# Loading the adjacency as int8 with converting GpSimd transfers, and a new split of the comparisons, in a graph-attention kernel

## The chip, the cores and the metric

The kernel runs on one core of one Trainium2 chip. The metric is device time in microseconds (us) of one execution. The kernel before takes 1601.66 us, the median of three runs (1600.64 to 1603.05). Its engines are TensorE (PE, with its weight loads apart as PEld), VectorE (DVE), ScalarE (ACT), GpSimd (POOL) and SyncE (SP), which here only issues transfers.

## The reference

One graph-attention layer with four heads of 32 outputs over 8192 nodes, then a residual and a layer norm without scale:

```python
Wh = (h @ W.T).reshape(n, K, OUT_DIM).transpose(1, 0, 2)      # n = 8192, K = 4, OUT_DIM = 32
e = jax.nn.leaky_relu(score_src + score_dst, 0.2)             # [K, n, n]
e = jnp.where((adj == 0)[None, :, :], -jnp.inf, e)
alpha = softmax(e, axis=-1)
h_prime = jnp.einsum('kij,kjd->kid', alpha, Wh)
x = _layernorm(x + h_prime.transpose(1, 0, 2).reshape(n, K * OUT_DIM), axis=-1)
```

`adj` is an int32 array of 8192 x 8192, whose values are 0 and 1 (268 MB; all of it must be read). `x` is 8192 x 128 fp32.

## The kernel before, in words

The exponential of a leaky ReLU of a sum splits into two products, one for a positive sum and one for a negative one. So no exponential is taken per edge: for every pair (i, j) and head only a bit is wanted, whether the sum is positive ("step") or not ("rest"), and the edge bit. TensorE then multiplies the step bits by table G and the rest bits by table F, both made once in the first 91 us.

**Tiling.** The rows i of the adjacency go in 16 groups of 512, and in each group the columns j in 16 "quads" of 512, 256 quads in all, numbered k. For one quad:

- SP loads the 512 x 512 block of int32 in two transfers of 128 partitions x 2 rows x 512 numbers (`load_adj`, L284) into one of two buffers `adj_t`. It waits for `edge_set`, which GpSimd raises when it has read that buffer.
- GpSimd turns the block into int8 with a clamp to -1..1 (`take_edges`, L351), into one of two buffers `edge`, and raises `edge_set`.
- TensorE transposes it (`transpose_edges`, 8 instructions, L770), two quads ahead of its use, into one of two PSUM banks, and raises `transposed`.
- The comparisons are 128x512 pieces, each with one head and one of four 128-row blocks. Heads 0 and 1 (`kept`, one of them kept from a group to the next) are ScalarE's alone: four instructions of double width (L471, 128x1024). Heads 2 and 3 make eight pieces, which `tiles(g, q)` deals out by `SHARES` as (ScalarE, GpSimd, VectorE): (2, 4, 2) in groups 1 to 14, (1, 5, 2) in group 0, (3, 4, 1) in group 15. ScalarE's are L471, GpSimd's L421, VectorE's L638.
- VectorE masks the step bits with the transposed edges (`take_step`: L650, L652 and L657; where it has a single piece of its own, L655 and L657) and makes the rest bits (`take_rest`: L665, L667). It makes its comparisons of quad k + 1 between the two.
- TensorE adds 64 products with G, then the transposes of quad k + 2, then 64 products with F (all L783), and raises `rest_done`.

**What sets the order.** Every engine's program is written out by hand, and semaphores couple them. GpSimd and ScalarE may be up to three quads ahead of TensorE (`NS = 3`, they wait for `rest_done`). VectorE's `take_step` waits for all three sharers of the quad. In GpSimd's program a quad is: its comparisons, `take_edges` for the quad two ahead, and in nine of the sixteen quads of a group one piece of closing work on the group before (`close` L363 to L387 and `inverse_deviation` L391). VectorE's closing work is `finish`, ScalarE's are L498 (accumulators copied out after quad 1) and L504. GpSimd's part of a quad:

```python
for n, h in tiles(g, q)[1]:
    last = nc.gpsimd.tensor_scalar(step_u8[...], s_own[...], STEEP, d_steep[...], ALU.mult, ALU.add)
last.then_inc(pool_compared, 1)
if k + N8 < GROUPS * QUADS:
    take_edges(k + N8)
if q in CLOSING and g > 0:
    close(g - 1, CLOSING.index(q))
```

Of the kernel before, what the change touches and what calls it, by code (L numbers as in the profile page):

```python
# [6 lines left out]
def gat_layernorm(nc, x, adj, W, a, out):  # L7
# [31 lines left out]
    JB = N // P  # L39
    XT = N // ROWS  # L40

    NA = 2
    N8 = 2
    NS = 3
    KEPT = 2
    PLACES = QUADS + NS
# [20 lines left out]


    TILES = [(0, 3), (1, 3), (0, 2), (1, 2), (2, 2), (3, 2), (2, 3), (3, 3)]
    SHARES = ((2, 4, 2),)  # L70

    def tiles(g, q):
        first_or_last = {0: (1, 5, 2), GROUPS - 1: (3, 4, 1)}
# [17 lines left out]
    with ctx:  # L91
# [8 lines left out]
        F = sb("F", [P, JB, HEADS, FP, HC], fp16)  # L100
        s_two = sb("s_two", [P, KEPT, 2, ROWS], fp32)
        s_own = sb("s_own", [P, 2, HEADS - KEPT, ROWS], fp32)
        adj_t = sb("adj_t", [P, NA, IB, ROWS], i32)
        edge = sb("edge", [P, N8, IB, ROWS], i8)
        kept = sb("kept", [P, PLACES + NS, WORDS], i32)
        step = sb("step", [P, NS, HEADS - KEPT, WORDS], i32)
# [89 lines left out]
        G1_set = sem("G1_set")  # L196
        G2_set = sem("G2_set")
        f_set = sem("f_set")
        adj_loaded = [sem(f"adj_loaded{n}") for n in range(NA)]
        edge_set = sem("edge_set")  # L200
        transposed = sem("transposed")
        act_compared = sem("act_compared")
        pool_compared = sem("pool_compared")
# [53 lines left out]
        @block.sync  # L257
        def _(sync):
            sync.sem_inc(stored, 16 * LEAD)
            sync.dma_start(w_sb, W[:, :]).then_inc(w_loaded, 16)  # L260
            for side in range(2):
                sync.dma_start(a_col[:, side:side + 1], a[:, side * D_OUT:(side + 1) * D_OUT].rearrange("h (c o) -> h c o", o=1)
                               ).then_inc(w_loaded, 16)
            for t in range(XT):
                sync.dma_start(blocks(x_sb[:, t]), x_v[t]).then_inc(x_loaded[t], 16)

            def load_s(g, h, to, loaded):
                sync.dma_start(to, sT_v[g, h].unsqueeze(0).to_broadcast([P, ROWS])).then_inc(loaded, 16)

            def load_own(g, h):  # L270
                load_s(g, h, s_own[:, g % 2, h - KEPT], own_loaded[g % 2])

            def load_two(g, later):

                if g + later < GROUPS:
                    load_s(g + later, g % 2, s_two[:, g % 2, 1 - later], two_loaded[g % 2])

            def load_adj(g, q):

                k = quad_no(g, q)  # L280
                if k >= NA:
                    sync.wait_ge(edge_set, k - NA + 1)
                for u in range(U):
                    sync.dma_start(adj_t[:, q % NA, u * E:(u + 1) * E], adj_v[g, q, :, u]).then_inc(adj_loaded[q % NA], 16)  # L284

            def store_rows(g):
                sync.wait_ge(y_set, done(g + 1))
                sync.dma_start(o_v[g], blocks(y)).then_inc(stored, 16)

            def load_rows(g):  # L290

                if g == 0:
                    sync.wait_ge(rest_done, QUADS)
                else:
                    sync.wait_ge(stored, 16 * done(g))
                sync.dma_start(blocks(y), x_v[g]).then_inc(res_loaded, 16)

            for g in range(GROUPS):
                for q in range(QUADS):
                    load_adj(g, q)  # L300
                    if g == 0 and q + 1 == NA:
                        for n in range(2):
                            sync.wait_ge(s_copied, n + 1)
                            sync.dma_start(sT_rows[n], s_rows[:, n]).then_inc(s_stored, 16)
                        sync.wait_ge(s_stored, 32)
                        load_s(0, 1, s_first, first_loaded)
                        load_two(0, 0)
                        load_two(0, 1)
                        load_own(0, 2)
                        load_own(0, 3)  # L310
                    if q == 4 and g > 1:
                        store_rows(g - 2)
                    if q == 7 and g > 0:
                        load_rows(g - 1)
                    if q in S_QUADS and g + 1 < GROUPS:

                        if g == 0:
                            sync.wait_ge(wide_set, UNITS)
                        else:
                            sync.wait_ge(rest_done, quad_no(g, 0))  # L320
                        n = S_QUADS.index(q)
                        if n < 2:
                            load_two(g + 1, n)
                        else:
                            load_own(g + 1, n)
            store_rows(GROUPS - 2)
            load_rows(GROUPS - 1)
            store_rows(GROUPS - 1)
            sync.wait_ge(stored, 16 * done(GROUPS))

        @block.gpsimd
        def _(pool):
# [10 lines left out]
            nc.gpsimd.affine_select(out=identf, in_=identf, compare_op=ALU.not_equal, fill=1.0,  # L343
                                    base=0, pattern=[[-1, P]], channel_multiplier=1).then_inc(consts_set, 1)

            def take_edges(k):

                pool.wait_ge(adj_loaded[k % NA], 16 * U * (k // NA + 1))
                if k >= N8:
                    pool.wait_ge(transposed, k - N8 + 1)  # L350
                nc.gpsimd.tensor_scalar(edge[:, k % N8], adj_t[:, k % NA], 1.0, -1.0, ALU.min, ALU.max).then_inc(edge_set, 1)  # L351

            def close(g, part):

# [35 lines left out]
                pool.wait_ge(var_set, done(g + 1))  # L390
                nc.gpsimd.tensor_tensor(rstd[:, :], mv[:, :, 1], half_t[:, :], ALU.pow).then_inc(rstd_set, 1)  # L391

            for k in range(N8):
                take_edges(k)
            pool.wait_ge(d_part_set, 1)
            nc.gpsimd.partition_all_reduce(d_max[:, :], d_part[:, :], P, bass.bass_isa.ReduceOp.max).then_inc(d_max_set, 1)
            pool.wait_ge(d_part_set, 2)
# [16 lines left out]
            for g in range(GROUPS):  # L414
                pool.wait_ge(own_loaded[g % 2], 32 * (g // 2 + 1))
                for q in range(QUADS):
                    k = quad_no(g, q)
                    if k >= NS:
                        pool.wait_ge(rest_done, k - NS + 1)
                    for n, h in tiles(g, q)[1]:  # L420
                        last = nc.gpsimd.tensor_scalar(step_u8[:, k % NS, h - KEPT, n // E, :, n % E], s_own[:, g % 2, h - KEPT],  # L421
                                                       STEEP, d_steep[:, q * IB + n, h:h + 1], ALU.mult, ALU.add)
                    last.then_inc(pool_compared, 1)
                    if k + N8 < GROUPS * QUADS:
                        take_edges(k + N8)
                    if q in CLOSING and g > 0:
                        close(g - 1, CLOSING.index(q))
                    if q == 13 and g > 0:
                        inverse_deviation(g - 1)
# [298 lines left out]
        def _(pe):  # L728
# [34 lines left out]
                nc.tensor.transpose(tr[n][:, 0:P], sd[:, 0, n * JB // 2:(n + 1) * JB // 2, :].rearrange("p j h -> p (j h)"), identf  # L763
                                    ).then_inc(sT_psum, 1)

            def transpose_edges(q):

                for u in range(U):
                    for b in range(IB):
                        last = nc.tensor.transpose(edgeT16[q % 2][:, u, b * P:(b + 1) * P],  # L770
                                                   edge16[:, q % N8, b, u * P:(u + 1) * P], identb[:, :])
                last.then_inc(transposed, 1)

            def add_quad(q, matrices, values, width, first, before=None, after=None):
# [26 lines left out]
            def group(g):  # L801
                for q in range(QUADS):
# [8 lines left out]
                             G, BC, 0, before=(lambda b: open_bank(g, b)) if q == 0 else None)  # L811
                    pe.wait_ge(rest_set, k + 1)
                    if k + 2 < GROUPS * QUADS:
                        pe.wait_ge(edge_set, k + 3)
                        transpose_edges(q + 2)
                    add_quad(q, [rest_f8[:, k % NL, n] for n in [n for _, n in two] + list(range(KEPT, HEADS))], F, FC, BC, after=close_bank if q + 1 == QUADS else None
                             ).then_inc(rest_done, 1)

            pe.wait_ge(s_copied, 2)
            for k in range(2):  # L820
                pe.wait_ge(edge_set, k + 1)
                transpose_edges(k)
            pe.wait_ge(G2_set, UNITS)
            pe.wait_ge(f_set, UNITS)
# [23 lines left out]
```

## Time and profile before

| | |
|---|---|
| runs | 1600.64, 1601.66, 1603.05 us |
| profiled execution, first to last instruction | 1599.2 us (no time of its own is listed apart from this span) |
| granted TensorE clock, mean | 0.976 |
| busy share PE, PEld, DVE, ACT, POOL | 89%, 87%, 97%, 94%, 86% |
| DMA | 303 MB, 189 GB/s over the span |
| chain that ended last | ACT 48%, DVE 29%, PE 14%, issue 5%, POOL 4% |
| groups 1 to 14 | 92.4 us each, 5.78 us for a quad |

The profile covers one execution. "Busy" counts the time in which an engine has an instruction under way; instructions of one engine overlap at their ends by some 0.03 to 0.09 us, so the price of an instruction in a row of its kind is the distance between starts, a little less than its duration. Granted clock 1.00 is 2.4 GHz and 0.50 is 1.2 GHz. Transfers that SP issues are shown as SPq.

### The profile page before, as it was taken

Reading aid. Unit: us, or ns where it says so; the run is one execution under the profiler, and the core shown is the slowest. Engines: PE = TensorE matmul, PEld = TensorE weight load, DVE = VectorE, ACT = ScalarE, POOL = GpSimd, SP = SyncE. Lnnn points to the kernel's source line nnn. Section 1 sums busy time; section 2 is a strip of 40 time slices with the busy share of each in tenths; the row PEclk is TensorE's granted clock in tenths of the full one; section 3 lists DMA queues with packets and bytes.
Section 4 is the critical chain, followed back from the end, with each engine's and each line's share of the span. In section 5 each row is a group of like instructions: output and inputs, shape, how many; then the busy total and the mean of one; then the engine's idle time right before and its main releaser. Section 6 shows DMA issues by size and latency. Waiting matters only on the chain.

```text
span 1599.2 us, 77812 instructions
## 1 busy us (share of the span) xinstructions
PE 1421.6 (89%) x35205; PEld 1388.1 (87%) x35205; DVE 1545.1 (97%) x2156; ACT 1496.1 (94%) x1834; POOL 1382.8 (86%) x1495
## 2 busy tenths in 40 slices
PE   6058999999999999999999999999999999999995
PEld 6048899989989999998999999898999989989995
DVE  7978999999999999999999999999999999999995
ACT  3799999999999999999999999999999999999883
POOL 1798898988989899898989899898989989998994
PEclk9579999999999999999999999999999999999998
DMA  4235565756666575666656666665666566565650
GB/s 161 88 118 183 179 213 172 232 184 194 212 194 213 173 234 193 203 194 211 207 179 220 196 203 200 200 220 174 225 200 199 190 204 232 170 212 188 200 187 22
DMA packets 162564, 303.01 MB, mean 189 GB/s; under 512 B 10296, under 2 KB 22968, under 8 KB 162232
## 3 DMA queue, kind: packets, MB, share of 16 engines
q1 hardware_dynamic: 162232, 298.03, 57.6%
q8 instruction: 276, 4.52, 1.1%
q14 instruction: 56, 0.46, 0.1%
HBM read 293.67 MB, written 4.33 MB: 186 GB/s over the span
## 4 chain that ended last, share of the span: by engine, by line
ACT 48%; DVE 29%; PE 14%; issue 5%; POOL 4%; DMA 0%; SPq 0%; POOLq 0%; DVEq 0%; ACTq 0%
ACT kept L471 35%; PE bank L783 12%; ACT step L471 9%; DVE rest L667 7%; DVE step L638 6%; DVE rest L665 5%; DVE kept L657 4%; DVE step L652 2%; ACT late L498 2%; PE bank L770 2%; ACT y L504 1%; POOL kept L407 1%; DVE step L650 1%; POOL G L411 1%; DVE stats L693 1%
## 5 line engine op out<-in xcount | busy, mean ns | idle before, releaser
L471 ACT ACTIVATE kept<-s_two,sd 128x1024 uint8<-128x1024 f32 (+1 forms) x1024 | 1066.7, 1122 | 39.4 <-PE bank L783 36.6
L421 POOL TENSOR_SCALAR step<-s_own,sd 128x512 uint8<-128x512 f32 x1040 | 704.7, 699 | 2.4
L783 PE MATMUL bank<-G,kept 128*128 128x99 bf16 x8192 | 535.9, 207 | 23.4 <-issue 14.6
L351 POOL TENSOR_SCALAR edge<-adj_t 128x2048 int8<-128x2048 int32 x256 | 485.2, 1895 | 77.3 <-PE bank L770 57.7
L783 PE MATMUL bank<-F,rest 128*128 128x66 f16 x16384 | 548.6, 194 | 3.0 <-issue 2.9
L783 PE MATMUL bank<-G,step 128*128 128x99 bf16 x8192 | 536.3, 207 | 9.6 <-issue 9.4
L783 PEld LDWEIGHTS bank<-F,rest 128*128 128x128 fp8e4 x16384 | 529.1, 98 | 2.9 <-issue 2.8
L783 PEld LDWEIGHTS bank<-G,kept 128*128 128x128 fp8e4 x8192 | 415.9, 97 | 31.1 <-issue 17.6
L783 PEld LDWEIGHTS bank<-G,step 128*128 128x128 fp8e4 x8192 | 420.2, 97 | 13.1 <-issue 12.8
L638 DVE SCALAR_TENSOR_TENSOR step<-s_own,sd,bank 128x512 uint8<-128x512 f32 x496 | 348.6, 746 | 7.0 <-PE bank L770 6.4
L471 ACT ACTIVATE step<-s_own,sd 128x512 uint8<-128x512 f32 x512 | 341.5, 721 | 0.0
L657 DVE SCALAR_TENSOR_TENSOR kept<-bank,kept 128x1024 int32<-128x1024 int32 x256 | 311.6, 1217 | 0.0
L667 DVE SCALAR_TENSOR_TENSOR rest<-kept,bank 128x1024 int32<-128x1024 int32 x256 | 311.6, 1217 | 0.0
L665 DVE SCALAR_TENSOR_TENSOR rest<-step,bank 128x1024 int32<-128x1024 int32 x256 | 311.6, 1217 | 0.0
L770 PE MATMUL bank<-identb,edge 128*128 128x128 bf16 x2048 | 158.5, 220 | 45.6 <-DVE rest L667 40.4
L770 PEld LDWEIGHTS bank<-identb,edge 128*128 128x128 bf16 x2048 | 119.2, 98 | 66.4 <-DVE rest L667 61.0
L652 DVE SCALAR_TENSOR_TENSOR step<-bank,step 128x512 int32<-128x512 int32 x240 | 164.1, 684 | 0.0
L650 DVE SCALAR_TENSOR_TENSOR step<-bank,step 128x256 int32<-128x256 int32 x240 | 100.4, 418 | 15.7 <-issue 9.7
L794 PE MATMUL bank<-zeros,identb 128*128 128x2 bf16 x96 | 16.1, 168 | 68.4 <-DVE kept L657 57.5
L794 PEld LDWEIGHTS bank<-zeros,identb 128*128 128x128 bf16 x96 | 9.5, 99 | 69.6 <-issue 69.6
L391 POOL TENSOR_TENSOR rstd<-mv,half_t 128x4 f32<-128x4 f32 x16 | 16.3, 1020 | 52.9 <-DVE mv L702 52.9
L381 POOL TENSOR_TENSOR late<-late,rden 128x512 f32<-128x512 f32 x16 | 17.0, 1065 | 42.3 <-DVE rden L688 42.3
(82 smaller groups left out, 549.9 us busy)
## 6 DMA issues: line engine op xcount, KB each, us to landing
adj_t<-in_adj SPq DMA_DIRECT2D x512, 512.0 KB, 4.8
s_own<-sT_scratch SPq DMA_DIRECT2D x32, 256.0 KB, 5.9
s_two<-sT_scratch SPq DMA_DIRECT2D x31, 256.0 KB, 5.1
kept<-in_x SPq DMA_DIRECT2D x16, 256.0 KB, 5.9
y<-in_x SPq DMA_DIRECT2D x16, 256.0 KB, 5.4
out<-y SPq DMA_DIRECT2D x16, 256.0 KB, 5.2
y<-sT_scratch SPq DMA_DIRECT2D x1, 256.0 KB, 3.8
sT_scratch<-late SPq DMA_DIRECT2D x2, 64.0 KB, 1.9
```

The costliest lines, as they stand in the source:

```text
L351: nc.gpsimd.tensor_scalar(edge[:, k % N8], adj_t[:, k % NA], 1.0, -1.0, ALU.min, ALU.max).then_inc(edge_set, 1)
L421: last = nc.gpsimd.tensor_scalar(step_u8[:, k % NS, h - KEPT, n // E, :, n % E], s_own[:, g % 2, h - KEPT], STEEP, d_steep[:, q * IB + n, ...
L471: return nc.scalar.activation(out, scores, ACT.Sigmoid, scale=STEEP, bias=d_steep[:, q * IB + b, h:h + 1])
L498: nc.scalar.copy(late[:, b * USED:b * USED + n_ch * CH], acc[b][:, 0:n_ch * CH]).then_inc(acc_act, 1)
L638: last = nc.vector.scalar_tensor_tensor(step_u8[:, k % NS, h - KEPT, b // E, :, b % E], s_own[:, g % 2, h - KEPT], d_neg[:, q * IB + b, h: ...
L650: nc.vector.scalar_tensor_tensor(step[:, k % NS, 1, 0:WORDS // U], edgeT[q % 2][:, 1, 0:WORDS // U], ONES, step[:, k % NS, 1, 0:WORDS // U ...
L652: nc.vector.scalar_tensor_tensor(step[:, k % NS, 0], edgeT[q % 2][:, 0], ONES, step[:, k % NS, 0], ALU.bitwise_and, ALU.bitwise_and)
L657: nc.vector.scalar_tensor_tensor(kept[:, both(k, k)[0]], edgeT[q % 2], ONES, kept[:, both(k, k)[0]], ALU.bitwise_and, ALU.bitwise_and).the ...
L665: nc.vector.scalar_tensor_tensor(rest[:, k % NL, KEPT:HEADS], step[:, k % NS], ONES, edgeT[q % 2], ALU.bitwise_xor, ALU.bitwise_and)
L667: nc.vector.scalar_tensor_tensor(rest[:, k % NL, 0:KEPT], kept[:, both(k, k)[0]], ONES, edgeT[q % 2], ALU.bitwise_xor, ALU.bitwise_and).th ...
L770: last = nc.tensor.transpose(edgeT16[q % 2][:, u, b * P:(b + 1) * P], edge16[:, q % N8, b, u * P:(u + 1) * P], identb[:, :])
L783: last = nc.tensor.matmul(acc[k][:, col:col + width], matrices[h][:, n // E, b * P:(b + 1) * P, n % E], values[:, q * IB + n, h].rearrange ...
```

## The change

The adjacency no longer goes through the int32 buffers. GpSimd's own queue issues the transfers, with the int8 buffer `edge` as destination, so that the transfer converts; there are four such buffers, loaded three quads ahead. The clamp is gone, and with it L351, `edge_set` and SP's adjacency transfers. TensorE waits for the transfers itself. In groups 1 to 14 the pieces of heads 2 and 3 are dealt (1, 6, 1).

```diff
-    NA = 2
-    N8 = 2
+    N8 = 4
...
-    SHARES = ((2, 4, 2),)
+    SHARES = ((1, 6, 1),)
...
-            def load_adj(g, q):
-                k = quad_no(g, q)
-                if k >= NA:
-                    sync.wait_ge(edge_set, k - NA + 1)
-                for u in range(U):
-                    sync.dma_start(adj_t[:, q % NA, u * E:(u + 1) * E], adj_v[g, q, :, u]).then_inc(adj_loaded[q % NA], 16)
...
-                    load_adj(g, q)
...
-            def take_edges(k):
-                pool.wait_ge(adj_loaded[k % NA], 16 * U * (k // NA + 1))
+            def load_edges(k):
+                g, q = k // QUADS, k % QUADS
                 if k >= N8:
                     pool.wait_ge(transposed, k - N8 + 1)
-                nc.gpsimd.tensor_scalar(edge[:, k % N8], adj_t[:, k % NA], 1.0, -1.0, ALU.min, ALU.max).then_inc(edge_set, 1)
+                for u in range(U):
+                    pool.dma_start(edge[:, k % N8, u * E:(u + 1) * E], adj_v[g, q, :, u]).then_inc(edge_loaded[k % N8], 16)
...
-            for k in range(N8):
-                take_edges(k)
+            for k in range(N8 - 1):
+                load_edges(k)
...
-                    if k + N8 < GROUPS * QUADS:
-                        take_edges(k + N8)
+                    if k + N8 - 1 < GROUPS * QUADS:
+                        load_edges(k + N8 - 1)
...
-            def transpose_edges(q):
+            def transpose_edges(k):
+                pe.wait_ge(edge_loaded[k % N8], 16 * U * (k // N8 + 1))
...
-                        pe.wait_ge(edge_set, k + 3)
-                        transpose_edges(q + 2)
+                        transpose_edges(k + 2)
```

GpSimd's program in a middle group, two quads of the kernel before: four comparisons and the conversion, the second quad with a piece of closing work.

```order
L421 TENSOR_SCALAR step<-s_own,sd 128x512 [waits rest_done]
L421 TENSOR_SCALAR step<-s_own,sd 128x512 x3
L351 TENSOR_SCALAR edge<-adj_t 128x2048 [waits transposed,adj_loaded0]
L421 TENSOR_SCALAR step<-s_own,sd 128x512 [waits rest_done]
L421 TENSOR_SCALAR step<-s_own,sd 128x512 x3
L351 TENSOR_SCALAR edge<-adj_t 128x2048 [waits transposed,adj_loaded1]
L381 TENSOR_TENSOR late<-late,rden 128x16x32 [waits rden_set]
```

The same two quads of the changed kernel, where L410 is the comparison, L340 the converting transfer and L370 what L381 was.

```order
L410 TENSOR_SCALAR step<-s_own,sd 128x512 [waits rest_done]
L410 TENSOR_SCALAR step<-s_own,sd 128x512 x5
L340 DMA edge<-in_adj 128x2x512 [waits transposed]
L340 DMA edge<-in_adj 128x2x512
L410 TENSOR_SCALAR step<-s_own,sd 128x512 [waits rest_done]
L410 TENSOR_SCALAR step<-s_own,sd 128x512 x5
L340 DMA edge<-in_adj 128x2x512 [waits transposed]
L340 DMA edge<-in_adj 128x2x512
L370 TENSOR_TENSOR late<-late,rden 128x16x32 [waits rden_set]
```

Two more comparisons stand in each quad, and two transfer issues where one conversion stood, in the same place behind the comparisons and ahead of the closing work. The wait for SP's transfer is gone.

VectorE's program for one quad of a middle group before: two masks of the step bits, the mask of the kept ones, two comparisons of the next quad, and the two rest instructions.

```order
L650 SCALAR_TENSOR_TENSOR step<-bank,step 128x256 [waits pool_compared,act_compared,dve_compared]
L652 SCALAR_TENSOR_TENSOR step<-bank,step 128x512
L657 SCALAR_TENSOR_TENSOR kept<-bank,kept 128x2x512
L638 SCALAR_TENSOR_TENSOR step<-s_own,sd,bank 128x512 [waits transposed]
L638 SCALAR_TENSOR_TENSOR step<-s_own,sd,bank 128x512
L665 SCALAR_TENSOR_TENSOR rest<-step,bank 128x1024 [waits rest_done,step_set]
L667 SCALAR_TENSOR_TENSOR rest<-kept,bank 128x1024
```

The same quad after: L644 is the mask, L646 that of the kept ones, L627 the comparison, L654 and L656 the rest.

```order
L644 SCALAR_TENSOR_TENSOR step<-bank,step 128x1024 [waits pool_compared,act_compared,dve_compared]
L646 SCALAR_TENSOR_TENSOR kept<-bank,kept 128x2x512
L627 SCALAR_TENSOR_TENSOR step<-s_own,sd,bank 128x512 [waits transposed]
L654 SCALAR_TENSOR_TENSOR rest<-step,bank 128x1024 [waits rest_done,step_set]
L656 SCALAR_TENSOR_TENSOR rest<-kept,bank 128x1024
```

One comparison is gone, and the two shorter masks (768 elements together) have become one of 1024, since a single own piece leaves too little masked beforehand.

## Rows read from the trace of the kernel before

**Rows 1.** The page: busy time and instructions of each engine, whole span.
```profile
PE 1421.6 (89%) x35205; PEld 1388.1 (87%) x35205; DVE 1545.1 (97%) x2156; ACT 1496.1 (94%) x1834; POOL 1382.8 (86%) x1495
```

**Rows 2.** Timeline of ACT (start us, us busy, engine, line): the accumulator copies.
```profile
291.47 2.60 ACT L498 COPY late<-bank 128x495 f32<-128x495 f32 x6
...
1493.02 2.62 ACT L498 COPY late<-bank 128x495 f32<-128x495 f32 x6
1579.59 2.67 ACT L498 COPY late<-bank 128x495 f32<-128x495 f32 x6 [7.75 <-PE bank L798]
```

**Rows 3.** Stretches: length, busy us of PE, PEld, DVE, ACT, POOL, clock, DMA share, GB/s.
```profile
11.50:20.00 8.50, 8.50 (x72) 8.50 (x72) 7.77 (x31) 3.51 (x6) 0.00 (x0) 1.00 1.08 366
...
97.90:190.00 92.10, 81.50 (x1961) 78.38 (x1962) 82.40 (x102) 91.94 (x109) 79.34 (x91) 0.98 0.57 186
291.50:1493.00 1201.50, 1130.57 (x28414) 1104.24 (x28415) 1195.18 (x1609) 1177.23 (x1381) 1076.72 (x1157) 1.00 0.63 201
1493.00:1579.60 86.60, 83.91 (x2161) 83.27 (x2158) 83.30 (x90) 65.74 (x110) 71.06 (x78) 1.00 0.48 155
```

**Rows 4.** Timeline of DVE, one quad of group 10.
```profile
1019.27 0.42 DVE L650 SCALAR_TENSOR_TENSOR step<-bank,step 128x256 int32<-128x256 int32 x1
...
1020.20 1.22 DVE L657 SCALAR_TENSOR_TENSOR kept<-bank,kept 128x1024 int32<-128x1024 int32 x1
1021.33 1.40 DVE L638 SCALAR_TENSOR_TENSOR step<-s_own,sd,bank 128x512 uint8<-128x512 f32 x2
1022.65 1.22 DVE L665 SCALAR_TENSOR_TENSOR rest<-step,bank 128x1024 int32<-128x1024 int32 x1
...
1024.91 0.42 DVE L650 SCALAR_TENSOR_TENSOR step<-bank,step 128x256 int32<-128x256 int32 x1
```

**Rows 5.** Timeline of ACT: two quads of group 0, and a quad of group 10.
```profile
95.33 4.26 ACT L471 ACTIVATE kept<-s_two,sd 128x1024 uint8<-128x1024 f32 x4
...
101.94 4.26 ACT L471 ACTIVATE kept<-s_two,sd 128x1024 uint8<-128x1024 f32 x4
...
1003.61 4.27 ACT L471 ACTIVATE kept<-s_two,sd 128x1024 uint8<-128x1024 f32 x4
1007.79 1.32 ACT L471 ACTIVATE step<-s_own,sd 128x512 uint8<-128x512 f32 x2
```

**Rows 6.** Timeline of POOL, one quad of group 1 with closing work.
```profile
206.40 2.72 POOL L421 TENSOR_SCALAR step<-s_own,sd 128x512 uint8<-128x512 f32 x4
209.08 1.90 POOL L351 TENSOR_SCALAR edge<-adj_t 128x2048 int8<-128x2048 int32 x1
...
212.06 2.71 POOL L421 TENSOR_SCALAR step<-s_own,sd 128x512 uint8<-128x512 f32 x4
```

**Rows 7.** Groups of POOL instructions: line, xcount, busy us, mean ns, idle before.
```profile
L351 POOL TENSOR_SCALAR edge<-adj_t 128x2048 int8<-128x2048 int32 x256 | 485.2, 1895 | 77.3 <-PE bank L770 57.7 <-DMA adj_t<-in_adj 19.2
...
L378 POOL TENSOR_TENSOR late<-late 128x528 f32<-128x528 f32 x16 | 21.6, 1348 | 0.1
...
L391 POOL TENSOR_TENSOR rstd<-mv,half_t 128x4 f32<-128x4 f32 x16 | 16.3, 1020 | 52.9 <-DVE mv L702 52.9
...
L837 POOL MEMSET const-float32-0.0<- 128x1 f32 x1 | 0.1, 98 | 0.2 <-issue 0.2
```

**Rows 8.** Timeline of PE in group 15: the transposes of two quads.
```profile
1515.61 0.61 PE L770 MATMUL bank<-identb,edge 128*128 128x128 bf16 x8
...
1557.70 0.61 PE L770 MATMUL bank<-identb,edge 128*128 128x128 bf16 x8
```

**Rows 9.** SP's issues of the adjacency transfers: duration ns min/median/max.
```profile
L284 SPq DMA_DIRECT2D adj_t<-in_adj x512: 539/606/1880, 11.5 to 1552.7; - x171
```

**Rows 10.** POOL comparisons in the first 91 us and later: duration ns min/median/max.
```profile
L407 POOL TENSOR_SCALAR kept<-y,sd x18: 684/1402/1411, 52.9 to 90.2; 128x512 uint8<-128x512 f32 x18
...
L421 POOL TENSOR_SCALAR step<-s_own,sd x1040: 684/696/740, 91.3 to 1568.6; 128x512 uint8<-128x512 f32 x174
```

**Rows 11.** DMA issues from 291.5 to 1493 us: xcount, KB each, us to landing.
```profile
adj_t<-in_adj SPq DMA_DIRECT2D x416, 512.0 KB, 4.8
```

More of the change, by code:

```diff
@@ L102, in gat_layernorm @@
         s_own = sb("s_own", [P, 2, HEADS - KEPT, ROWS], fp32)
-        adj_t = sb("adj_t", [P, NA, IB, ROWS], i32)
         edge = sb("edge", [P, N8, IB, ROWS], i8)
@@ L198, in gat_layernorm @@
         f_set = sem("f_set")
-        adj_loaded = [sem(f"adj_loaded{n}") for n in range(NA)]
-        edge_set = sem("edge_set")
+        edge_loaded = [sem(f"edge_loaded{n}") for n in range(N8)]
         transposed = sem("transposed")
@@ L299, in _ @@
                 for q in range(QUADS):
-                    load_adj(g, q)
-                    if g == 0 and q + 1 == NA:
+                    if g == 0 and q == 1:
                         for n in range(2):
@@ L764, in _ @@
                                     ).then_inc(sT_psum, 1)
-            def transpose_edges(q):
+            def transpose_edges(k):
+                pe.wait_ge(edge_loaded[k % N8], 16 * U * (k // N8 + 1))
                 for u in range(U):
                     for b in range(IB):
-                        last = nc.tensor.transpose(edgeT16[q % 2][:, u, b * P:(b + 1) * P],
-                                                   edge16[:, q % N8, b, u * P:(u + 1) * P], identb[:, :])
+                        last = nc.tensor.transpose(edgeT16[k % 2][:, u, b * P:(b + 1) * P],
+                                                   edge16[:, k % N8, b, u * P:(u + 1) * P], identb[:, :])
                 last.then_inc(transposed, 1)
@@ L820, in _ @@
             for k in range(2):
-                pe.wait_ge(edge_set, k + 1)
                 transpose_edges(k)
```

## The prediction

> **What bounds the kernel now.** I read the shares of the page first. All five rows stand between 86% and 97% [rows 1]; that tells only that no engine has much room. So I went to the copies of the accumulators on ScalarE, one in each group, as a ruler: from 291.47 to 1493.02 us lie 13 groups, 92.43 us each, or 5.78 us for a quad, and group 15, which has VectorE's share at one piece already, took 86.6 us from its predecessor's copy to its own [rows 2]. The same two stretches by engine show VectorE busy 1195 of 1201.5 us in the middle groups and ScalarE 1177, while in group 15 TensorE leads with 83.9 of 86.6 us [rows 3].
>
> The timeline of VectorE gives its quad: from one first mask to the next 5.64 us without a hole [rows 4]. Sixteen of them are 90.2 us; the other 2.2 us of a group are its closing work and small waits. ScalarE's quad is 4.18 us for the four wide comparisons and 0.66 us for each narrow one [rows 5], 5.50 us with two; with its copies, 2.6 us in a group [rows 2], it is a close second. GpSimd's quad is 2.68 us for four comparisons, 1.9 us for the conversion, and in nine quads of sixteen about 1.1 us of closing work [rows 6]. GpSimd is not the bound: it waits for TensorE ahead of the conversion 57.7 us in all [rows 7].
>
> **The change, engine by engine, for one middle group.**
>
> VectorE loses one comparison (1.32 us for two from start to start, so 0.66) and its masks of 0.93 us become one of 1024 elements at 1.13 us, the distance from L657 to the next start [rows 4]. That is -0.66 + 0.20 = -0.46 us in a quad, -7.4 us in a group: 92.4 becomes 85.0 us.
>
> ScalarE loses a narrow comparison: 4.84 us in a quad [rows 5], 77.4 us in a group, and with some 4 us of copies and scaling 82 us.
>
> TensorE's instructions stay. Its floor is seen in group 15: eight quads in 42.09 us, 5.26 each [rows 8], 84.2 us in a group. So what these three allow is the pace of group 15, where VectorE has the same program: 86.6 us, 5.8 us less than now. For 14 groups that is -82 us, if GpSimd and the transfers keep up.
>
> GpSimd gets six comparisons: 6 x 0.67 = 4.02 us in a quad [rows 6], 64.3 us in a group. The closing work stays: nine instructions in a group whose means add up to 10.3 us, the dearest 1.35 and the cheapest 1.02 us [rows 7]. The conversion of 1.90 us goes, and two transfer issues of d us each come in its place, 32 in a group. Its group is thus 74.6 + 32 d. Issues stand in the same in-order program as the comparisons, so what an issue takes of GpSimd delays the next quad's comparisons, for which VectorE's first mask waits, and behind that TensorE. Three step buffers let GpSimd run ahead, which evens out the quads with closing work but gives no pace. Against 92.43 us now the break-even is d = 17.8 / 32 = 0.557 us; down to d = 0.375 us GpSimd sets the pace, below that group 15's pace does. Everything hangs on d.
>
> **What an issue costs.** The trace has no transfer issued by GpSimd. From below: its shortest instruction takes 0.098 us [rows 7]. From above: the longest of SP's issues of this same 128x2x512 transfer, 1.88 us, which is also about what the conversion takes (1.895 us) [rows 7, 9]. Between them lie SP's usual issue of this shape, 0.606 us [rows 9], and GpSimd's dispatch of an instruction of almost no work, four numbers in each partition, 1.02 us [rows 7]. SP hands the 256 rows of a transfer to hardware, and even that takes more than the break-even. GpSimd has to work them out itself, with no 128 lanes to help it: its 2048 elements against 512 cost 1.895 - 0.699 us, 0.79 ns an element, and 0.29 us remain as fixed part. If one row of the transfer costs as much as one such element, d is 0.29 + 256 x 0.79 ns = 0.49 us; at four elements a row, 1.1 us. I take d = 1.0 us, nearest to the 1.02 us row.
>
> The Trainium skill speaks on both sides here and no run here shows it yet. "DMA: Bandwidth & Descriptors", section "Latency and other measured facts", puts the first byte of a transfer from GpSimd's software path at about 1 us and calls that the emission overhead; by it the estimate would be d = 1.0 too. The same page, "Anatomy of one DMA", calls descriptor generation small and says many descriptors can be emitted before their cost shows; by that d would be below the break-even and the 82 us would come. The rows above neither have a GpSimd issue nor exclude this, which is why the second case below keeps a quarter.
>
> **The other terms.** Group 0 keeps its shares. ScalarE paces it, 6.61 us a quad [rows 5]; GpSimd there would need 5 x 0.67 + 2 d = 5.35 us at d = 1.0, so nothing changes (from d = 1.63 it would). Group 15: 16 x 2.68 + 10.3 + 26 issues of d = 79.2 us, still under its 86.6. Start: three quads of adjacency now leave GpSimd's queue from the third microsecond on, beside x, while SP issued two behind x. Transfers moved 366 GB/s from 11.5 to 20 us with TensorE busy throughout [rows 3]; shared, x can come late by 0 to 4 us, and I take 1. SP loses its 512 issues and keeps the small ones, which no longer stand behind adjacency waits: nothing. The wait for the transfer moves from GpSimd to TensorE. It is issued three quads ahead, over 15 us, and landed in 4.8 us [rows 11]; what stands behind it on TensorE is the F product, but it is not reached. TensorE's clock: group 0 runs at 6.61 us a quad, TensorE's 5.26 being 80% of it, at clock 0.98 [rows 3], the upper level of 2.4 GHz; the forecast's 6.66 us is the same picture, so I charge nothing.
>
> **Sum.** At d = 1.0 a middle group takes 74.6 + 32.0 = 106.6 us against 92.43: +14.2 us, 14 times, +198; with the start +199. The profiled span is 1599.2 us, 2.5 us under the median of 1601.66; the difference goes on that median: 1801 us. In general 1353 + 448 d us for d over 0.375.
>
> **Rivals.**
>
> 1. *A cheap issue, d under 0.5 us.* GpSimd drops out and group 15's pace rules: 14 x -5.8 + 1 gives 1521 us for d up to 0.375, and 1577 at 0.5. For it: the one-element-a-row working above. Against it: SP's 0.606 us.
> 2. *An issue like SP's, d from 0.5 to 0.62 us.* The gain on VectorE and the issues cancel: 1577 to 1631 us, 1625 at 0.606.
> 3. *The conversion slows the transfer engines.* The middle groups move 201 GB/s at a share of 0.63, of which the adjacency is 416 x 0.524 MB in 1201.5 us, 181 GB/s [rows 3, 11]. That is 0.63 x 5.78 = 3.64 us of transfer time a quad, 3.28 of it adjacency. If converting doubles this the quad needs 6.9 us whatever GpSimd does: 110.7 us a group, 14 x 18.3 = +256, group 0 +5, group 15 +20: about 1883 us. It decides from a factor of 1.65 on. For it: 512 bytes are written for every 2048 read, in a form this trace never shows. Against it: the bytes read are the same, and the engines have reached 366 GB/s.
> 4. *VectorE locks GpSimd's descriptor writes out.* In the first 91 us GpSimd's comparison took 1.40 us, twice the later 0.70 [rows 10], beside VectorE instructions that read two operands from SBUF; all 1040 later ones lie between 0.684 and 0.740 us. The steady VectorE program has one SBUF operand each and moves 1024 elements in 1.13 us, so I see no such lock there; if each issue waited half a VectorE instruction, d = 1.57 us and 2056 us. The Trainium skill, "SBUF — State Buffer", section "SBUF: two separate sides", warns of just this for instructions in a two-port mode; the trace agrees that a lock exists in the first stretch and shows none later.
>
> **How the numbers follow.** Forecast (d from 0.62 to 1.9) 0.53; rival 1, 0.25; rival 2, 0.07; rival 3, 0.12; rival 4, 0.03. Forecast's own range: d from 0.8 to 1.3 us, 1711 to 1935 us. The range must reach rival 1's 1521 us, which holds a quarter: low 1515; above, d = 1.42 us or rival 3 with a factor just above 2.1 gives 1990, beyond which I leave some 0.13. About 0.2% of the time, 3 us, is what can be told from no change. Slower: 0.53 + 0.12 + 0.03 + 0.02 from rival 2 = 0.70. The same: 0.02, since d would have to lie within 0.007 us of break-even. Faster: 0.25 + 0.03 = 0.28.
>
> **What would show it.** GpSimd's comparisons of consecutive quads standing 4.02 us plus 2 d apart, with no idle time on it and gaps of about 1 us between a quad's last comparison and the next; VectorE's first mask (now L644) waiting for GpSimd's L410 in most quads, and a busy share of VectorE near 80%. In rival 1 TensorE's transposes would stand 5.26 us apart and GpSimd would wait for `rest_done`. In rival 3 TensorE's transposes would wait for the transfer `edge<-in_adj`, landing in over 15 us, at a DMA share near 1. The forecast is wrong if a GpSimd issue holds the engine for less than 0.557 us.

## The result, and the profile after

The changed kernel takes 1675.86 us (1675.34 to 1675.92, four runs) against 1602.36 us beside it: a ratio of 1.0458, 95% interval [1.0446, 1.0471]. It is slower, by 73.5 us where 199 were forecast (37% of it); the time lies inside the range given.

Of the page after: the engines' busy times, the first shares of the chain that ended last, and the costliest groups that answer to [rows 1] and [rows 7] (line, engine, operation, names, shapes, xcount | busy us, mean ns | idle before, releaser).

```profile
PE 1431.2 (86%) x35205; PEld 1398.3 (84%) x35205; DVE 1466.8 (88%) x1708; ACT 1371.7 (82%) x1610; POOL 1574.3 (94%) x2199
...
POOL 77%; PE 9%; ACT 6%; DVE 5%; issue 3%; DMA 0%; SPq 0%; POOLq 0%; ACTq 0%; DVEq 0%
...
L410 POOL TENSOR_SCALAR step<-s_own,sd 128x512 uint8<-128x512 f32 x1488 | 1002.9, 686 | 25.3 <-PE bank L773 20.3
...
L644 DVE SCALAR_TENSOR_TENSOR step<-bank,step 128x1024 int32<-128x1024 int32 x240 | 292.7, 1219 | 152.0 <-POOL step L410 150.0
...
L340 POOL DMA_DIRECT2D edge<-in_adj x512 | 376.8, 736 | 0.4
```

Before, GpSimd had 4% of that chain; now it has 77%. VectorE's first mask (L644) waits 150 us for GpSimd's comparisons, in 145 of its 240 quads. The transfer issues (L340) are on GpSimd as busy time: 377 us, where the conversion had 485.

The timeline of GpSimd after, two quads of a middle group; it answers to [rows 6].

```profile
1005.86 4.04 POOL L410 TENSOR_SCALAR step<-s_own,sd 128x512 uint8<-128x512 f32 x6
1009.85 1.48 POOL L340 DMA_DIRECT2D edge<-in_adj  x2
1011.36 1.15 POOL L360 TENSOR_TENSOR late<-late 128x528 f32<-128x528 f32 x1
1012.50 4.05 POOL L410 TENSOR_SCALAR step<-s_own,sd 128x512 uint8<-128x512 f32 x6
```

From the start of the comparisons to that of the issues are 3.99 us, and from there to the closing work 1.51 us: an issue holds GpSimd for 0.755 us. Over the kernel it is 0.75, which is used below; its duration alone reads 0.72 us. There is no hole on the engine. The issues answer to SP's [rows 9] and the copies of the accumulators, the ruler of the groups, to [rows 2]:

```profile
L340 POOL DMA_DIRECT2D edge<-in_adj x512: 713/722/934, 2.7 to 1628.9; - x171
```

```profile
200.03 2.62 ACT L487 COPY late<-bank 128x495 f32<-128x495 f32 x6
...
294.13 2.62 ACT L487 COPY late<-bank 128x495 f32<-128x495 f32 x6
...
1471.85 2.62 ACT L487 COPY late<-bank 128x495 f32<-128x495 f32 x6
...
1569.51 2.62 ACT L487 COPY late<-bank 128x495 f32<-128x495 f32 x6
```

From 294.13 to 1471.85 lie 12 groups, 98.14 us each, where 92.43 stood. GpSimd's sum gives the same: 16 x 3.99 + 10.1 + 32 x 0.75 = 97.9 us, the 10.1 being the closing work from start to start. Up to the first copy the kernel lost 1.05 us against 198.98 us before; GpSimd's first comparison of the quads already starts 1.7 us later (92.96 against 91.3 us). The stretch from the first to the last of these copies is 1369.5 against 1294.0 us (+75.4), and the end is 2.3 us shorter: +74.2 us, the difference of the spans 1673.4 and 1599.2.

### The profile page after: what moved, and what is told of

It reads as the page before. It is cut to its first block, busy times and chain, and to the rows that moved or that the text cites. A ratio compares the mean times of both kernels' runs of the same rounds, so it can differ in the third digit from the quotient of the medians.

```text
span 1673.4 us, 77078 instructions
## 1 busy us (share of the span) xinstructions
PE 1431.2 (86%) x35205; PEld 1398.3 (84%) x35205; DVE 1466.8 (88%) x1708; ACT 1371.7 (82%) x1610; POOL 1574.3 (94%) x2199
## 4 chain that ended last, share of the span: by engine, by line
POOL 77%; PE 9%; ACT 6%; DVE 5%; issue 3%; DMA 0%; SPq 0%; POOLq 0%; ACTq 0%; DVEq 0%
POOL step L410 49%; POOL edge L340 17%; PE bank L773 8%; ACT kept L460 5%; POOL late L367 1%; POOL kept L396 1%; POOL y L376 1%; POOL late L363 1%; POOL late L370 1%; POOL late L360 1%; POOL late L352 1%; POOL late L354 1%; POOL late L357 1%; POOL G L400 1%; POOL rstd L380 1%
## 5 line engine op out<-in xcount | busy, mean ns | idle before, releaser
L410 POOL TENSOR_SCALAR step<-s_own,sd 128x512 uint8<-128x512 f32 x1488 | 1002.9, 686 | 25.3 <-PE bank L773 20.3
L644 DVE SCALAR_TENSOR_TENSOR step<-bank,step 128x1024 int32<-128x1024 int32 x240 | 292.7, 1219 | 152.0 <-POOL step L410 150.0
L340 POOL DMA_DIRECT2D edge<-in_adj x512 | 376.8, 736 | 0.4
L646 DVE SCALAR_TENSOR_TENSOR kept<-bank,kept 128x1024 int32<-128x1024 int32 x256 | 310.8, 1214 | 0.0
L654 DVE SCALAR_TENSOR_TENSOR rest<-step,bank 128x1024 int32<-128x1024 int32 x256 | 310.8, 1214 | 0.0
L656 DVE SCALAR_TENSOR_TENSOR rest<-kept,bank 128x1024 int32<-128x1024 int32 x256 | 310.8, 1214 | 0.0
L627 DVE SCALAR_TENSOR_TENSOR step<-s_own,sd,bank 128x512 uint8<-128x512 f32 x272 | 200.3, 742 | 6.5 <-PE bank L760 6.4
L460 ACT ACTIVATE step<-s_own,sd 128x512 uint8<-128x512 f32 x288 | 202.0, 712 | 0.0
L487 ACT COPY late<-bank 128x495 f32<-128x495 f32 x96 | 42.0, 529 | 7.4 <-PE bank L788 7.4
L493 ACT ACTIVATE y<-y,shift,rstd 128x128 f32<-128x128 f32 x64 | 26.2, 480 | 12.7 <-DVE shift L696 12.7
L400 POOL TENSOR_TENSOR G<-late,G 128x396 bf16<-128x396 f32 (+1 forms) x22 | 20.0, 909 | 11.7 <-issue 7.4
```

Of the source, the lines that this page charges most:

```text
L340: pool.dma_start(edge[:, k % N8, u * E:(u + 1) * E], adj_v[g, q, :, u]).then_inc(edge_loaded[k % N8], 16)
L400: nc.gpsimd.tensor_tensor(G[:, blk, :, 2, :], left[:, m % NU, 0:blk.stop - blk.start], G[:, blk, :, 1, :], ALU.subtract).then_inc(G2_set, 1)
L460: return nc.scalar.activation(out, scores, ACT.Sigmoid, scale=STEEP, bias=d_steep[:, q * IB + b, h:h + 1])
L487: nc.scalar.copy(late[:, b * USED:b * USED + n_ch * CH], acc[b][:, 0:n_ch * CH]).then_inc(acc_act, 1)
L627: last = nc.vector.scalar_tensor_tensor(step_u8[:, k % NS, h - KEPT, b // E, :, b % E], s_own[:, g % 2, h - KEPT], d_neg[:, q * IB + b, h: ...
L644: nc.vector.scalar_tensor_tensor(step[:, k % NS], edgeT[q % 2], ONES, step[:, k % NS], ALU.bitwise_and, ALU.bitwise_and)
```

## The experiments

All times stand beside the kernel before on the same chip (1600.9 to 1602.4 us in median). The group times are taken from the copies of the accumulators, as above, over 11 to 13 groups.

**The converting transfers alone.** The changed kernel with the old split:

```diff
-    SHARES = ((1, 6, 1),)
+    SHARES = ((2, 4, 2),)
```

> The changed kernel with the old split (2, 4, 2) in groups 1 to 14, so the converting transfers alone. Theory A (the busiest engine sets the pace, and an issue holds GpSimd for 0.752 us and does nothing else): GpSimd needs 16 x 4 x 0.667 + 10.1 + 32 x 0.752 = 76.8 us a group and is off the path; VectorE's 92.2 us stays: 1595 to 1604 us. Theory B (the converting transfers cost something beside GpSimd's time, as a later arrival or a slowed engine): over 1612 us, with TensorE waiting for edge<-in_adj.

Measured: 1607.56 us, ratio 1.0035 [1.0016, 1.0055]. GpSimd is busy 80% and off the path, so this is nearer to theory A, but 3.6 us above its range, and between the two theories. TensorE never waits for the transfer. A group takes 92.9 us against 92.4, and the first copy stands 2.8 us later than before (201.75 against 198.98). TensorE's pauses that no releaser explains, stretches without work and without a semaphore to wait for, are listed by the profile as `issue`. Here are the costliest waits that bear on it (engine, line <- cause: us, times, longest), 303 to 1400 us.

```profile
PEld bank L760 <- DVE rest L656: 55.2, 117, 0.7
PE bank L760 <- DVE rest L656: 36.8, 106, 0.6
ACT kept L460 <- PE bank L773: 21.8, 30, 2.7
PEld bank L773 <- issue: 20.4, 23, 2.9
```

The longest pause, 2.9 us, is twice the longest in the same kind of row before (1.5 us), but the pauses of TensorE's matmuls sum to no more than before (20 against 21 us in this stretch). So no run shows what the 0.35% are made of; it is small beside the rest.

**The split alone.** The kernel before, conversion on GpSimd:

```diff
-    SHARES = ((2, 4, 2),)
+    SHARES = ((1, 6, 1),)
```

> The kernel before with the new split (1, 6, 1), so the shares alone, conversion still on GpSimd. Theory A: GpSimd needs 16 x 6 x 0.667 + 10.1 + 16 x 1.88 = 104.2 us a group against 92.4: 1602 + 14 x 11.8, less some 4 us for the lead it has from group 0, 1763 us. If instead GpSimd's time were not what sets the pace of the changed kernel, this would stay near the changed kernel's 1676 us.

Measured: 1773.19 us, ratio 1.1071 [1.1038, 1.1105], where 1763 was expected; 105.0 us a group against 104.2 from the sum. So the split alone costs 172 us, and on top of it the transfers give 97 back. GpSimd's time sets the pace in both; the chain that ended last here:

```profile
POOL 75%; issue 10%; PE 6%; ACT 6%; DVE 3%; DMA 0%; SPq 0%; POOLq 0%; ACTq 0%; DVEq 0%
```

**GpSimd relieved.** Two of its six comparisons left out in groups 1 to 14, so that the step bits are incomplete; the other engines' programs are unchanged:

```diff
-        return act, [t for t in left if t not in act], own
+        pool = [t for t in left if t not in act]
+        return act, pool if g in first_or_last else pool[:4], own
```

> The changed kernel with two of GpSimd's six comparisons in groups 1 to 14 left out (those pieces of the step bits are not made). VectorE's, ScalarE's and TensorE's programs are those of the changed kernel. Theory A: GpSimd needs 76.8 us a group, and the pace of group 15, 86.6 us, shows: 1521 us. If the transfers or TensorE's new wait set a pace of their own, it stays above 1560 us.

Measured: 1534.87 us, ratio 0.9590 [0.9554, 0.9627], 87.8 us a group in place of 86.6. This is what rival 1 promised, 14 us dearer (1521 us expected). From 303 to 1400 us TensorE is busy 1066 of 1097 us and stands 23 us in pauses without a releaser. These are hardly more than the 21 us of the kernel before, but there VectorE set the pace (busy 1091 of the same 1097 us) and covered them.

**Four issues a quad.** The same bytes in transfers of 128 rows:

```diff
-                for u in range(U):
-                    pool.dma_start(edge[:, k % N8, u * E:(u + 1) * E], adj_v[g, q, :, u]).then_inc(edge_loaded[k % N8], 16)
+                for b in range(IB):
+                    pool.dma_start(edge[:, k % N8, b], adj_v[g, q, :, b // E, b % E]).then_inc(edge_loaded[k % N8], 16)
```

> The changed kernel with a quad's adjacency in four transfers of 128 rows x 512 in place of two of 256 rows. Theory F (the price of an issue is mostly fixed): 4 x 0.7 in place of 2 x 0.752 us, GpSimd's group 98.1 + 16 x 1.3 = 119 us, about 1676 + 290 = 1965 us, and also groups 0 and 15 grow. Theory R (it goes by rows): 128 rows cost 0.38 us, the time stays near 1676 us. Half fixed (0.38 us + 1.45 ns a row): 0.56 us an issue, 4 x 0.56 - 1.50 = +0.74 us a quad, 1676 + 14 x 11.8 = 1841 us.

Measured: 1839.11 us, ratio 1.1480 [1.1459, 1.1501]: the case "half fixed", within 2 us. GpSimd's timeline there:

```profile
1008.90 2.20 POOL L340 DMA_DIRECT2D edge<-in_adj  x4
1011.09 1.38 POOL L367 TENSOR_TENSOR late<-late 128x528 f32<-128x528 f32 x1
```

Four issues take 2.19 us, 0.548 each. With 0.75 for 256 rows that is 1.6 ns a row and 0.34 us fixed, a line through two points; the group is 109.3 us, the sum 64.0 + 10.1 + 64 x 0.548 = 109.2.

**Longer rows.** The adjacency of two quads in one pair of transfers, 256 rows of 1024 numbers, half the issues:

```diff
-                for u in range(U):
-                    pool.dma_start(edge[:, k % N8, u * E:(u + 1) * E], adj_v[g, q, :, u]).then_inc(edge_loaded[k % N8], 16)
+                for u in range(U):
+                    pool.dma_start(edge2[:, j % 2, u * E:(u + 1) * E], adj_v2[g, q // 2, :, u]).then_inc(edge_loaded[j % 2], 16)
...
-                    if k + N8 - 1 < GROUPS * QUADS:
-                        load_edges(k + N8 - 1)
+                    if k % 2 == 1 and k + N8 - 1 < GROUPS * QUADS:
+                        load_edges((k + N8 - 1) // 2)
```

> The changed kernel with the adjacency of two quads in one pair of transfers, 256 rows x 1024 columns each: half the issues, the same bytes. If an issue's price does not depend on the row's length (0.752 us), GpSimd's group is 64.0 + 10.1 + 12.0 = 86.1 us and the floor of group 15's pace, 86.6 to 88 us, shows: 1521 to 1545 us, faster than both kernels with the split (1, 6, 1) itself. If it goes by bytes (1.5 us an issue), nothing is won: 1676 us.

Measured: 1575.67 us, ratio 0.9832 [0.9811, 0.9854]. The issues and their durations:

```profile
L341 POOL DMA_DIRECT2D edge<-in_adj x256: 713/726/934, 2.7 to 1523.6; - x128
```

The price does not move with the bytes (median 726 ns, against 722), and GpSimd leaves the path: 100 us less than the changed kernel. The chain that ended last:

```profile
PE 65%; POOL 14%; ACT 7%; DVE 7%; issue 5%; DMA 1%; SPq 0%; POOLq 0%; ACTq 0%; DVEq 0%
```

But 90.0 us a group is not the 86 to 88 expected. TensorE accounts for it: its pauses are 51 us from 303 to 1400 us (47 ahead of products, 4 ahead of transposes), against 23 with GpSimd relieved, 2.2 us a group more, and 2.2 us is what a group takes more. The start lost another 4.5 us (first copy at 205.06 against 200.58 us). One pause:

```profile
1008.74 0.30 PE L774 MATMUL bank<-G,step 128*128 128x99 bf16 x3
1010.32 0.38 PE L774 MATMUL bank<-G,step 128*128 128x99 bf16 x5 [1.28 <-issue]
```

It stops in the middle of eight products that need nothing new. The stretches around it (us, busy PE, PEld, DVE, ACT, POOL, clock, DMA share, GB/s) show the transfer engines full for most of it; what TensorE waits for there comes below ("What the pauses hang on"):

```profile
1008.00:1009.00 1.00, 1.00 (x24) 0.93 (x21) 1.00 (x2) 1.00 (x3) 1.00 (x2) 1.00 1.09 147
1009.00:1010.00 1.00, 0.04 (x1) 0.00 (x0) 1.00 (x2) 1.00 (x3) 1.00 (x3) 1.00 1.10 111
1010.00:1011.00 1.00, 0.68 (x14) 0.68 (x14) 0.49 (x1) 1.00 (x2) 1.00 (x2) 1.00 0.58 53
```

**Without conversion.** The same transfers from GpSimd, int32 to int32; TensorE transposes zeros, so the edge mask is not applied:

```diff
-                    pool.dma_start(edge[:, k % N8, u * E:(u + 1) * E], adj_v[g, q, :, u]).then_inc(edge_loaded[k % N8], 16)
+                    pool.dma_start(raw[:, k % 2, u * E:(u + 1) * E], adj_v[g, q, :, u]).then_inc(edge_loaded[k % N8], 16)
```

> The changed kernel with the same transfers issued by GpSimd but without conversion, int32 to an int32 buffer that nobody reads; TensorE transposes a buffer of zeros, so the edge mask is not applied. If the conversion has no part in the price of an issue and none in the transfer engines' time, 0.752 us and a DMA share near 0.56 for GpSimd's queue remain, 1676 us. If conversion makes an issue dearer, say twice a plain one at 0.38 us, GpSimd's group is 86 us and the time near 1521 us.

Measured: 1679.99 us, ratio 1.0486 [1.0463, 1.0509]; an issue reads 740 ns in the mean against 736. Conversion has no part in the issue's price. The transfer engines' time does differ: the queue of the changed kernel first, that of this run second (packets, MB, share of 16 engines).

```profile
q0 software_dynamic: 139264, 67.14, 55.5%
```

```profile
q0 software_dynamic: 73728, 268.47, 46.6%
```

Of their spans these shares are 929 and 782 us: the converting transfers take 1.19 times the transfer engines' time of the plain ones for the same reads. Rival 3 needed 1.65. How much of the 19% is the conversion itself is not shown, for the converting queue also has 1.9 times the packets. The run with longer rows has 69632 packets for the same converted bytes, and its share of 53.0% is 834 us, 1.07 times the plain ones; but the same number of packets reads 902 us in the spread run below, so these times also depend on how the transfers follow each other.

**Balanced.** The changed kernel with its eight pieces dealt so that GpSimd has five:

```diff
-    SHARES = ((1, 6, 1),)
+    SHARES = ((2, 5, 1), (1, 5, 2))
```

> The changed kernel with the split (2, 5, 1) in even quads and (1, 5, 2) in odd ones. Theory A: GpSimd 53.4 + 10.1 + 24.1 = 87.6 us a group, VectorE the mean of 92.4 and 85.0 = 88.7, ScalarE the mean of 92 and 82 = 87: about 88.7 to 89.5 us, 1550 to 1562 us, faster than both kernels. Rival: the engines can't even out quads of two kinds, each quad goes by its slower engine: VectorE and ScalarE at their 5.64 and 5.5 us quads in turn, 92 us a group, about 1600 us.

Measured: 1570.25 us, ratio 0.9791 [0.9752, 0.9830], 90.6 us a group; later, beside the last experiment, 1571.86 us, 0.9810 [0.9784, 0.9836]. The engines do even out quads of two kinds. The rest above 1550 to 1562 us fits TensorE's pauses, 28 and 34 us in the 1097 us of the two traces, but that they are all of it is not shown.

> The balanced kernel once more, on the chip of the run before, for comparison: 1570 us as before, within 5 us; the ratio to the kernel before near 0.979.

**Pairs and balanced together.**

> Transfers of two quads as in the run with pairs, and the split (2, 5, 1) and (1, 5, 2) in turn. GpSimd needs 53.4 + 10.1 + 12.0 = 75.5 us a group and is off the path; VectorE's mean of 88.7 us sets the pace: 1550 to 1560 us, so slower than the run with pairs and (1, 6, 1) where GpSimd takes 86.1 us, if issues cost the same at any row length; faster than it, if they go by bytes.

Measured: 1594.29 us, ratio 0.9942 [0.9914, 0.9970]. Slower than the run with pairs, as said, but also than the balanced one, and 34 us above the 1550 to 1560 us: two helps that relieve the same engine don't add up, and with the transfers of 4 KB rows TensorE stands 58 us in pauses from 200 to 1500 us here too (59 us in the run with pairs, 27 with GpSimd relieved).

**What the pauses hang on.** Three buffers of two quads, and one transfer a quad (the cut shows the issuing lines against the run with pairs):

```diff
-                    if k % 2 == 1 and k + N8 - 1 < GROUPS * QUADS:
-                        load_edges((k + N8 - 1) // 2)
+                    if k // 2 + 2 < GROUPS * QUADS // 2:
+                        load_edges(k // 2 + 2, (k % 2,))
```

> Transfers of two quads' columns as in the run with pairs, three buffers of two quads in place of two, and one transfer issued in each quad, in place of two back to back in every second one. Split (1, 6, 1). GpSimd's group is 86.1 us as there. In the run with pairs TensorE stood still without a releaser for 53 us between 200 and 1500 us (25 us in the kernel before), in stretches where the transfer engines were full. Theory A (a burst of 2 MB holds up something that TensorE needs, half the burst holds it up less): these pauses fall to 25 us or less and the time to 1535 to 1555 us. Theory B (the pauses come from 4 KB rows, or the time lost is the wait for `transposed` of two buffers): B1, pauses stay near 53 us and the time near 1575 us; B2, the time falls, but so it does in the run with three buffers and no spreading.

and the same three buffers without the spreading:

> As the run with pairs, two transfers back to back in every second quad, but three buffers of two quads, so that GpSimd need not wait for `transposed`. It tells the buffers' part from the spreading's: theory A and B1, the pauses stay near 53 us and the time at 1568 to 1577 us; theory B2, 1535 to 1555 us.

Measured: 1603.31 us spread, ratio 1.0023 [0.9999, 1.0046], and 1575.37 us unspread, 0.9840 [0.9814, 0.9867]. All three expectations fail for the spread run: it is the slowest. The buffers give nothing. TensorE's pauses from 303 to 1400 us in three kernels, first GpSimd relieved (2 KB rows, two transfers a quad), then pairs, then pairs spread:

```profile
PE bank L774 <- issue: 21.4, 26, 2.4
```

```profile
PE bank L774 <- issue: 46.8, 61, 2.3
```

```profile
PE bank L774 <- issue: 63.4, 69, 2.4
```

A quad's bytes are the same in all three. The pauses are 2.2 times as many us with rows of 4 KB in bursts and 3 times with the same transfers spread evenly, so the size of the burst is not it. Between the last two runs the pauses grow by 14 us in this stretch and the groups by 26, so they are only about half of what the spread run loses there.

What TensorE waits for in a pause is its own program. The traces have a queue for instructions, here that of the changed kernel (packets, MB, share of 16 engines); its packets and MB are the same in all 14 kernels:

```profile
q8 instruction: 276, 4.52, 1.1%
```

These are 276 blocks of 16 KB, and the trace holds 70717 instructions of TensorE (matmuls, weight loads and 307 others), 256.2 for each block. Counting them from the first, all 494 pauses of its matmuls from 303 to 1400 us, in the 14 kernels together, fall on the border between two blocks, 256 instructions or a multiple of it apart. Each ends 1.20 to 1.66 us after a block has landed. Of the 891 waits with a named releaser 7 fall on a border and 12% end at such a distance. The pause of 1.28 us above ends 1.47 us after the block that landed at 1008.85.

The blocks come late beside the adjacency. A block's transfer starts at most 276 instructions before TensorE needs it; in the median it is 190 with GpSimd relieved, 158 with pairs and 143 spread. It mostly starts when a burst ends: with GpSimd relieved 27 packets of the other queues are under way in the 0.9 us before (median) and 4 in the 0.7 us after, with pairs 18 and 3. That the bursts hold the blocks up is read from this and not tested by a run, and why spreading the transfers makes them later stays open.

**A version that beats both.** The balanced kernel with GpSimd given one more piece in group 0, ScalarE none (the cut leaves out the lines that move ScalarE's semaphore to its last comparison):

```diff
-        first_or_last = {0: (1, 5, 2), GROUPS - 1: (3, 4, 1)}
+        first_or_last = {0: (0, 6, 2), GROUPS - 1: (3, 4, 1)}
```

> The balanced kernel (converting transfers, (2, 5, 1) and (1, 5, 2) in turn) with group 0 dealt (0, 6, 2) in place of (1, 5, 2). In group 0 ScalarE paces with 6.61 us a quad; it loses one narrow comparison of 0.66 us: 5.95 us against GpSimd's 6 x 0.667 + 2 x 0.752 = 5.5 us and VectorE's 5.64 us. Theory A (pace of the busiest): 16 x 0.66 = 10.6 us less than the balanced kernel, about 0.65%: some 1560 us. Rival: GpSimd loses the lead over TensorE that group 0 gives it, and the later groups give back 4 us or more: under 7 us less.

Measured: 1562.12 us, ratio 0.9754 [0.9731, 0.9776], 9.7 us under the balanced kernel beside it (theory A said 10.6). The first copies of the accumulators, here and in the balanced kernel:

```profile
193.01 2.63 ACT L487 COPY late<-bank 128x495 f32<-128x495 f32 x6
```

```profile
200.78 2.63 ACT L487 COPY late<-bank 128x495 f32<-128x495 f32 x6
```

7.8 us are won up to this copy, where theory A had 10.6; the other 2 us are within what the two kernels' runs differ by among themselves. GpSimd's waits for TensorE up to there fall from 20 to 2.5 us, so it gives up some of its lead, and it is not missed.

## Why the prediction was right in direction and wrong in size

The step that failed is the price of an issue: "I take d = 1.0 us, nearest to the 1.02 us row." It is 0.75 us. The sum itself held: 1353 + 448 d gives 1689 us at 0.75, 13 above the measured time.

Point by point:

- *GpSimd's group.* Forecast 106.6, measured 98.14 us. Of the 8.5 us, 32 x 0.25 = 8.0 are d; the rest is that comparisons and closing work were taken a little long. Over 14 groups that is 118 us of the miss of 125. Another 4 us: the first of these groups took 94.1 us, since GpSimd came into it ahead (in group 0 it waited 20 us for TensorE's `rest_done`), which the sum didn't credit. The end gave 2.3 us more.
- *The choice of the row.* GpSimd's instruction on four numbers (1.02 us) is a power, no measure of a dispatch; its memset of the same four numbers takes 0.10 us and its two small reductions 0.39 and 0.44 us. The working with fixed part and rows was closer in form than the row that I chose by: 0.29 us and 0.79 ns a row stood there, 0.34 us and 1.6 ns a row were measured, so two elements a row, 0.70 us, would have been near. SP's 0.606 us for the same shape [rows 9] was the nearer row: with it 1625 us.
- *Where it decides.* Break-even at 0.557 us was right as far as the runs reach: with half the issues (0.376 us for each old one) the same split is faster by 1.7%, with 0.75 slower by 4.6%, with 1.10 (four of 0.548) by 14.8%.
- *VectorE, ScalarE, TensorE.* The relieved kernel shows 87.8 us a group where the sum had 86.6. TensorE's pauses are not this difference: they are 1.9 us a group there, and group 15 of the kernel before, from which the 86.6 come, holds 2.6 us of them. From the end of one TensorE group to the next that group took 87.2 us; the copies as a ruler read it 0.6 us short. The rest is that TensorE is busy 85.4 us in a middle group of the relieved kernel and 84.5 in group 15, whose last two quads have no transposes to make.
- *Rival 1* fell with d. Its floor was 14 us too low. *Rival 2's* 1625 us at SP's price was the nearest of the single times, 51 us off; the measured d of 0.75 lies above its stretch and below the forecast's own 0.8 to 1.3.
- *Rival 3*: the factor is 1.19, not 1.65. The 1.65 holds against the pace of before; against the forecast's own 6.66 us a quad the prediction's terms give 1.92. *Rival 4*: the issues lie between 713 and 934 ns with VectorE busy 88% of the span; no lock shows.
- *The Trainium skill*, "DMA: Bandwidth & Descriptors": taken as engine time, the first-byte figure of about 1 us in "Latency and other measured facts" is 0.25 us more than measured; no run here shows the first byte itself. "Anatomy of one DMA" calls descriptor generation small and lets many descriptors pass before their cost shows. Here 128 rows more cost GpSimd 0.2 us.
- *The start* came out as taken: +1.05 us to the first copy for 1. Other runs with transfers of 2 KB rows and the same group 0 stand 1.4 to 2.8 us behind the kernel before at this copy, so that it came so near is partly luck.
- *The signs named* came: 4 us and 2 d from one quad's comparisons to the next (plus closing work), no idle time on GpSimd, VectorE waiting for L410. The gap between a quad's last comparison and the next is 2 d or more, 1.5 us, and not the 1 us said. VectorE's busy share is 88%, where 80% was said, as d is smaller.

## What to carry to other kernels

A transfer moved to GpSimd's queue is not free for GpSimd: here 0.55 us for 128 rows and 0.75 for 256, the same for 2 and 4 KB rows and with or without conversion. Count it as an instruction of the engine before giving that engine more work; the transfers were worth 97 us and the split cost 172, and one piece fewer for GpSimd turned +4.6% into -2% (-2.5% with group 0 dealt anew). Few long rows make the issues cheaper, but check what they do to the engine that has the least slack: here the transfers go with later blocks of TensorE's own program, and an engine with a program of 70,000 instructions needs a new block every 5 to 6 us.

## What was not expected of the hardware

- TensorE stops for up to 3.5 us at the borders of the 16 KB blocks in which its program arrives: its matmuls stand 21 us in 1097 us in the kernel before, where VectorE covers it, 23 with converting transfers of 2 KB rows and GpSimd relieved, 51 with 4 KB rows and 65 with these spread.
- Transfers that convert int32 to int8 take the transfer engines 19% more time than plain ones, in 1.9 times the packets, though they write a quarter of the bytes.
- Two transfers of 1 MB back to back in every second quad end up 28 us better than one in every quad (1575.4 against 1603.3 us).
